# Edge stage of a graph kernel: GpSimd takes the three products of the third weight of each fourth tile, VectorE takes back the two of the first weights

## What is computed

```python
h = edge_attr_8                                   # [40000, 8]
for W in (W_mlp1, W_mlp2, W_mlp3):
    h = SILU_2MOM * silu(h @ W / sqrt(W.shape[0]))
w1, w2, w3, w4 = split(h @ W_mlp4 / 8, 4)         # 4 weights of 128 per edge
s0, s1 = x0[sender], x1[sender]                   # [E,128], [E,128,3]
p1 = w1 * s0 * y0                                 # y0, y1: edge_attr_4
p2 = (w2 * s0)[:, :, None] * y1[:, None, :]
p3 = w3[:, :, None] * s1 * y0[:, None, :]
p4 = w4 * einsum('eum,em->eu', s1, y1) / sqrt(3)
msg0 = segment_sum(concat([p1, p4]), receiver)    # per node
msg1 = segment_sum(concat([p2, p3]), receiver)
```

## Time and profile before

| | us |
|---|---|
| median of three runs | 1516.37 |
| the profiled execution, its own time | 1517.24 |
| span of its trace | 1515.4 |
| edge stage in it: first messages to last closing | 865.3 to 1372.1 |

### The profile page before, as it was taken

One profiled execution on the slowest core, in us unless ns is written; L12 is line 12 of the kernel. 1 busy time (PEld: TensorE's weight loads), 2 busy tenths in 40 slices (PEclk: granted clock), 3 DMA queues, 4 the chain that ended last, 5 costly groups with the idle time before them and its releaser, 6 DMA issues. The chain is left out here.

```text
span 1515.4 us, 26210 instructions
## 1 busy us (share of the span) xinstructions
PE 1378.3 (91%) x8774; PEld 837.2 (55%) x8774; DVE 1207.7 (80%) x1633; ACT 1026.6 (68%) x2442; POOL 990.2 (65%) x850
## 2 busy tenths in 40 slices
PE   5858989998899989999896899999999999988998
PEld 3545737885388846887384533333333333336786
DVE  7888818995299936998198499999999999995464
ACT  6347718884288825887183689989989888883343
POOL 4136647888688888888871278878887888772000
PEclk9859999999899999999999999999999999999999
DMA  9338393559445955473523588888888888885321
GB/s 338 133 154 269 106 372 87 162 175 381 125 134 166 346 191 176 138 261 110 184 52 122 174 263 274 285 277 277 277 283 265 277 272 279 277 269 171 115 86 56
DMA packets 90990, 316.66 MB, mean 209 GB/s; under 512 B 23642, under 2 KB 25876, under 8 KB 80747
## 3 DMA queue, kind: packets, MB, share of 16 engines
q1 hardware_dynamic: 45208, 202.57, 36.1%
q0 software_dynamic: 45648, 112.41, 27.8%
HBM read 378.96 MB, written 77.16 MB: 301 GB/s over the span
## 5 line engine op out<-in xcount | busy, mean ns | idle before, releaser
L1883 POOL DMA_INDIRECT sorted_edges<-arena x320 | 473.3, 1479 | 105.5 <-issue 97.7
L898 DVE TENSOR_TENSOR weights_hl<-arena,weights_hl 128x1024 fp32r<-128x1024 f32 x342 | 405.2, 1222 | 62.4 <-ACT weights_hl L1222 59.7
L1930 POOL DMA_INDIRECT arena<-node_table,arena x352 | 337.5, 959 | 135.2 <-issue 40.5
L1222 ACT ACTIVATE weights_hl<-arena 128x1024 fp32r<-128x1024 f32 x342 | 351.9, 1059 | 46.7 <-PE pair L1582 46.5
L1380 ACT ACTIVATE arena<-arena 128x32 f32<-128x32 bf16 x1408 | 359.0, 342 | 2.1 <-DVE arena L1008 2.1
L1582 PE MATMUL pair<-weights_hl,rows_hl 128*128 128x512 f32 x1368 | 326.2, 396 | 4.4 <-DVE rows_hl L903 1.7
L1029 DVE TENSOR_TENSOR arena<-pair,arena 128x768 f32<-128x768 f32 x352 | 317.9, 942 | 0.0
L1582 PEld LDWEIGHTS pair<-weights_hl,rows_hl 128*128 128x128 f32 x1368 | 251.8, 188 | 70.1 <-DVE weights_hl L898 10.6
L1719 PE MATMUL pair<-arena 64*128 64x512 f32 x704 | 189.8, 627 | 24.2 <-DVE arena L1029 23.4
L1582 PE MATMUL pair<-weights_hl,hidden_hl 128*128 128x512 f32 x684 | 165.8, 396 | 0.0
L917 DVE TENSOR_TENSOR arena<-pair,arena 128x512 f32<-128x512 f32 x69 | 47.3, 685 | 125.3 <-ACT arena L1260 97.5
(11 more groups left out here) (289 smaller groups left out, 1531.4 us busy)
## 6 DMA issues: line engine op xcount, KB each, us to landing
arena<-in_w SPq DMA_DIRECT2D x77, 2048.0 KB, 11.5
arena<-in_w SPq DMA_DIRECT2D x77, 1024.0 KB, 8.3
sums<-arena SPq DMA_DIRECT2D x88, 512.0 KB, 6.9
other_down<-in_w SPq DMA_DIRECT2D x8, 1024.0 KB, 10.4
arena<-in_v SPq DMA_DIRECT2D x16, 512.0 KB, 4.6
pair_rows<-arena SPq DMA_DIRECT2D x1, 5934.0 KB, 26.3
arena<-pair_rows SPq DMA_DIRECT2D x23, 256.0 KB, 3.5
arena<-node_table,arena POOLq DMA_INDIRECT x352, 4.8
```

Of the source, the lines that this page charges most:

```text
L898: v.tensor_tensor(out=part[s][:, 1], in0=by_chunk(n)[4], in1=part[s][:, 0].bitcast(F32), op=ALU.subtract).then_inc(v_low, 1)
L1222: a.activation(out=part[s][:, 0], in_=cols, func=ACT.Copy).then_inc(a_high, 1)
L1883: g.indirect_dma_start(out=sorted_edges, out_offset=bass.IndirectOffsetOnAxis(ap=slot_i[:, j:j + 1], axis=0), in_=er[:, j, :], in_offset=N ...
L1930: g.indirect_dma_start(out=row, out_offset=None, in_=table, in_offset=bass.IndirectOffsetOnAxis(ap=senders[:, i:i + 1], axis=0)).then_inc( ...
```

## The change

The fourth tile's products are dealt out otherwise. GpSimd makes the three products of w3 (384 values) in place of the two of w1 and w2 (256 values). VectorE's first operation of h = 1 covers both tiles (512 values in place of 256), and its last one makes only the three products of w4 (384 values in place of 768). ScalarE copies one weight (128 values) in place of two. VectorE's wait for `a_wcopy` moves from ahead of the last operation of h = 1 to ahead of its first.

```diff
@@ messages_of(s, h), VectorE @@
                 if s >= 2:
                     v.wait_ge(p_sum, s - 1)
-                n = 2 - h
-                v.tensor_tensor(out=m[:, 0:n, 0:2],
-                                in0=tp[:, :].rearrange("p (t w u) -> p t w u", t=2, w=4)[:, 0:n, 0:2],
-                                in1=rows_in[:, 0:n, 0:1].to_broadcast([128, n, 2, MUL]), op=ALU.mult)
+                if h:
+                    v.wait_ge(a_wcopy, s + 1)
+                v.tensor_tensor(out=m[:, :, 0:2],
+                                in0=tp[:, :].rearrange("p (t w u) -> p t w u", t=2, w=4)[:, :, 0:2],
+                                in1=rows_in[:, :, 0:1].to_broadcast([128, 2, 2, MUL]), op=ALU.mult)
                 for t in range(2):
-                    if h and t:
-                        v.wait_ge(a_wcopy, s + 1)
-                    w34 = tp[:, t * 512 + 256:(t + 1) * 512].rearrange("p (w u) -> p w u", w=2)
-                    v.tensor_tensor(out=m[:, t, 2:8].rearrange("p (w m) u -> p w m u", w=2),
-                                    in0=w34.unsqueeze(2).to_broadcast([128, 2, 3, MUL]),
-                                    in1=rows_in[:, t, 1:4].unsqueeze(1).to_broadcast([128, 2, 3, MUL]),
+                    w = 1 if h and t else 2
+                    w34 = tp[:, t * 512 + (4 - w) * MUL:(t + 1) * 512].rearrange("p (w u) -> p w u", w=w)
+                    v.tensor_tensor(out=m[:, t, 8 - 3 * w:8].rearrange("p (w m) u -> p w m u", w=w),
+                                    in0=w34.unsqueeze(2).to_broadcast([128, w, 3, MUL]),
+                                    in1=rows_in[:, t, 1:4].unsqueeze(1).to_broadcast([128, w, 3, MUL]),
                                     op=ALU.mult).then_inc(v_msg, 1)
@@ copy_weights(s), ScalarE @@
-                a.activation(out=w_copy[s % 2], in_=tp_bank[Q - 1][:, 0:2 * MUL], func=ACT.Copy).then_inc(a_wcopy, 1)
+                a.activation(out=w_copy[s % 2], in_=tp_bank[Q - 1][:, 2 * MUL:3 * MUL], func=ACT.Copy).then_inc(a_wcopy, 1)
@@ products_of(s), GpSimd @@
-                g.tensor_tensor(out=msg_pair[s % 2 * 2 + 1][:, 1, 0:2],
-                                in0=w_copy[s % 2].rearrange("p (w u) -> p w u", w=2),
-                                in1=gat_pair[i % NGAT // 2][:, 1, 0:1].to_broadcast([128, 2, MUL]), op=ALU.mult
-                                ).then_inc(g_msg, 1)
+                g.tensor_tensor(out=msg_pair[s % 2 * 2 + 1][:, 1, 2:5],
+                                in0=w_copy[s % 2].unsqueeze(1).to_broadcast([128, 3, MUL]),
+                                in1=gat_pair[i % NGAT // 2][:, 1, 1:4], op=ALU.mult).then_inc(g_msg, 1)
```

More of the change, by code:

```diff
@@ L307, in program @@
         *sums_in, w_copy0, w_copy1 = phase_tensors(**{f"sums_in{i}": (8 * MUL, F32) for i in range(3)},
-                                                   edge_weights0=(2 * MUL, F32), edge_weights1=(2 * MUL, F32))
+                                                   edge_weights0=(MUL, F32), edge_weights1=(MUL, F32))
         w_copy = (w_copy0, w_copy1)
```

## The result

| | before | changed |
|---|---|---|
| median, lowest and highest of 5 runs, us | 1519.14 (1516.31 to 1521.02) | 1542.3 (1540.05 to 1543.67) |
| the profiled execution, its own time | 1517.24 | 1541.15 |
| span of its trace | 1515.4 | 1539.4 |

The ratio is 1.0156, 95% interval 1.0142 to 1.0169: 1.6% slower, between the medians 23.2 us. The forecast was +22.6. The forecast median of 1539.0 started from 1516.4 for the kernel before; its median of five runs is 2.8 us higher, and that is most of the distance from 1539.0 to 1542.3.

What follows compares the result with a forecast made beforehand. VectorE and GpSimd were both taken as full at 5.66 us a step, with GpSimd pacing after the change. Products +23.7, tail -0.4, collisions -0.7 gave +22.6 on 1516.4: 1539.0 us, range 1533.0 to 1545.0.

Steps and rivals of the forecast that it cites:

- The bound: Edge stage: GpSimd, at 5.66 us a step, is as full as VectorE, its 0.30 us pauses its own; step becomes 5.94.
- itself never waited: Edge stage: GpSimd never waited for VectorE, so the buffers' lead for VectorE doesn't enter the sum.
- The price of a product: GpSimd's products, 256 to 384 values: 0.275 us more each, between 0.26 and 0.32; 86 of them, +23.7 us.
- the far bound of 0.11: GpSimd's 128 more values at the copies' slope, 0.11 us a product; as a rival about 1524.8 us, chance 0.05.
- 0.60 and 0.465: VectorE's h = 1: first operation 0.33 to 0.60 us, last one 0.865 to 0.465; together -0.13 us a step.
- Its busy share: VectorE in an edge-stage stretch: busy share falls to about 93%, idle time ended by gathers, weights or sums.
- The moved wait: VectorE's wait for `a_wcopy` ahead of h = 1: costs 0; as a rival that it bites, 1548 us, chance 0.03.
- Its cover: From the end of ScalarE's copy (1002.48) to the start of VectorE's h = 1 (1004.55): 2.07 us hide the moved wait.
- The tail: End of the edge stage: VectorE stands ready, begins with the last landing, and its h = 1 is 0.13 shorter: -0.4 us.
- Collisions: VectorE's comparisons meeting GpSimd's products: -0.7 us, half the possible gain, as most comparisons should fall among the gathers.
- the best case of the bounds: Collisions: no comparison meets GpSimd's products any more, -1.4 us; if all do, +3.2.

Runs made afterwards that it cites:

- gp512_light: Changed kernel with half of TensorE's sum left out and GpSimd's products at 512 values in place of 384, into a scratch tile: 1558.56 us, 1.0266 of before.

## Why the prediction was right, point by point

**The bound.** The step of the argument that carried all the rest, that GpSimd has no slack although the page has it idle for a third, held. On the first kind of chip 0.27 more in each product moved the step by 0.27 twice, from 5.66 to 5.93 and from 5.93 to 6.20, the second time with every other engine idling. The pauses of 0.30 didn't shrink when VectorE had time to spare, and neither did the longest, which stood in the earlier trace rows. Timeline of the changed kernel:

```profile
1176.60 1.41 DVE L1029 TENSOR_TENSOR arena<-pair,arena 128x768 f32<-128x768 f32 x2
...
1184.85 0.96 POOL L1929 DMA_INDIRECT arena<-node_table,arena  x1 [2.20 <-DVE arena L1029]
```

The messages that this gather needs were done at 1178.01, 6.8 us ahead of it. The pause stands ahead of the same gather, the 220th, in all fourteen traces, with 2.19 or 2.20 us each time, whichever engine had time to spare; nobody's wait does that. What GpSimd does in it isn't shown. The forecast's "itself never waited" is true of the stage but not of its opening: the ninth gather of the changed kernel waits 0.6 us for the first messages, and two of the kernel before waited 0.16 each.

**The price of a product.** Taken: 0.275 between bounds of 0.26 and 0.32, measured 0.268, and the far bound of 0.11 fell. By four sizes the line is 0.20 us and 2.1 ns a value. From the 4497 ns that the Trainium skill, GPSIMD Engine Reference, section 3.1, gives for 2048 values I had an estimate of 0.27 for these 128; the trace agrees with it.

**VectorE.** Taken: 0.60 and 0.465, measured 0.60 and 0.465. Its busy share, forecast as about 93%, is 93.8 to 96.1. Its waits in the stage are 19.3 us for landings (10.9 of them ahead of the first messages) and 19.0 us for the weights of TensorE, none for ScalarE's copy.

**The moved wait.** Costed at nothing, and nothing it cost. Its cover was 2.07 us in the step of the rows and is smaller now, 1.10 (copy done at 1001.92, h = 1 at 1003.02), which the prediction hadn't said. Over all steps its median went from 1.71 to 0.89 us, and behind the opening it never is under 0.70.

**The tail.** Taken: -0.4, measured 22.54 - 23.33 = -0.8, and here the mechanism was wrong. VectorE was to stand ready and begin with the landing. But the last landing, seen in the start of the last products, comes 4.80 us behind the last gather, where it was 6.13, and finds VectorE in its messages of h = 0; h = 1 begins at 1387.58, 0.93 later, where it was 0.26. The landing gives -1.3, VectorE's lateness +0.7, its shorter h = 1 -0.1. That the two unforeseen terms left a sum near the forecast was luck.

**Collisions.** Taken: -0.7, and this is the term that was mis-sized: it had the wrong victim. No product is lengthened any more (-1.4, the best case of the bounds). But twelve gathers are, each by 0.21 us. Timeline of the changed kernel:

```profile
1052.51 1.27 DVE L1041 SCALAR_TENSOR_TENSOR arena<-arena,pair 128x1024 f32<-128x1024 f32 x1
1053.70 0.42 DVE L1008 TENSOR_TENSOR arena<-arena 128x512 bf16<-128x512 bf16 x1
...
1053.79 1.15 POOL L1929 DMA_INDIRECT arena<-node_table,arena  x1 [0.30 <-issue]
```

The gather begins 0.09 us behind the comparison and takes 1.15 in place of 0.95. That is 12 x 0.21 = +2.5, so collisions cost +1.1 and not -0.7. I had put the comparisons among the gathers and thought that a gather is safe from them. One that is already under way is: with its start 0.05 us ahead of the comparison at 1223.21 it took its usual 0.95. The Trainium skill, SBUF — State Buffer, "Who interferes with whom", says that two SBUF inputs contend with a GpSimd instruction that reads SBUF, and infers that a `tensor_tensor` leaves descriptor generation alone; the rows agree with the first and not with the second. The indices of these gathers lie in SBUF (`senders` in the kernel), which may be the reason; that wasn't tested.

**The sum.** 86 x 0.269 (by the means without the long ones) = 23.1, collisions +1.1, the other gathers -0.5 in all, GpSimd's odd pauses -0.1, the first gather -0.3 (at 857.28, before at 857.56), tail -0.8: 22.5, the 22.54 of the last closing. Behind the stage come 1.4 us for the clock, which the sum didn't have, and it ends at +24.0 for the span. Against the forecast's terms the products missed by -0.6, collisions by +1.8, the tail by -0.4, the small terms by -0.9 and the clock by +1.4, and they partly cancelled; the median's +23.2 is nearer to +22.6 than the parts deserved. The products alone carry the result: no other line of the sum is over 1.4 us.

**Where it would have been wrong.** On the second kind of chip the same edit gains 2.8%. Nothing in the trace of before could tell that, since TensorE doesn't stop in it. The verdict holds for chips on which the kernel before takes 1519 us.

## What to carry to other kernels

An engine that issues indirect gathers can be full at 65% busy: compare its distance from step to step with the sum of its records and pauses, and if the pauses keep their size in a stage where nobody can hold it up, every value moved onto it is paid in full. Moving 0.13 us off one full engine onto another that pays 0.27 for it loses. And run the kernel before beside each experiment: where it doesn't come back to its old time, the chip has another bound, and the size of a change, even its sign, is that chip's alone.

## What the runs showed of the hardware that was not expected

- A comparison on VectorE with two bf16 inputs in SBUF lengthens a gather of GpSimd that begins shortly behind it: from 0.95 to 1.15 to 1.20 us when the gather begins 0.05 to 0.09 us behind it in the changed kernel. Over all traces a gather that began 0.03 to 0.26 us behind a comparison ended 1.24 to 1.27 us behind the comparison's start, wherever between them it began.
- Products of GpSimd behind a comparison can hold up VectorE instead. A comparison that began 0.28 us ahead of the products took 1.57 us in place of 0.41, and they their usual 1.00; one 0.04 us ahead of them took 1.34. In the kernel before such a meeting had cost both sides 0.23. Timeline of the changed kernel:

```profile
935.33 1.57 DVE L1008 TENSOR_TENSOR arena<-arena 128x512 bf16<-128x512 bf16 x1
...
935.61 1.00 POOL L1919 TENSOR_TENSOR arena<-edge_weights,arena 128x384 f32<-128x384 f32 x1
```

- Sixteen products of TensorE behind 3 us with 1.06 us of work ran mostly at the 1.2 GHz level in one trace, 3.41 us for what took 2.05, and at 2.4 GHz in two others (the kernel before, `gp512_light`) behind as little work.
- GpSimd's pause of 2.19 to 2.20 us ahead of the 220th gather of the stage, in every trace, whatever the other engines do.
- Two kinds of chip: the kernel before takes 1515 to 1524 us on one and 1616 to 1635 on the other. Nearly the whole difference is in the edge stage (first messages to last closing 505.5 against 608.1 us, 102.6 of the 108.8 us between the two spans), where TensorE's signals come late and its records have gaps of 1.5 to 3.4 us. A slower rhythm of the other engines takes about half of it back (1574 to 1580 us with the changed kernel and more work on VectorE).
